# Expert loop of a decoder layer: larger rings for gathered rows and outputs, kept in another buffer, and the last routed groups' sends placed earlier

## Chip, cores and metric

The kernel runs on one core of a Trainium2 chip. The metric is device time in microseconds (us) of one execution; the figure of a kernel is the median of its runs. The engines of the core are named as the profile names them: PE (matmul; PEld its weight loads), DVE (vector), ACT (scalar), POOL (GpSimd) and SP, which here only issues DMAs.

## What is computed

64 sequences of 64 tokens, 128 features each, in float32. Three stages, each added to its input and layer-normed: causal self-attention with 16 query heads and one key/value head, cross-attention on a context of 96 features, and a mixture of experts in which each token goes to two of eight experts. The change is in the third stage. Its reference, shortened:

```python
scores = einsum('bsd,nd->bsn', x, Wr) + br
w = softmax(scores)
_, idx = top_k(scores + biases_N, 2)
val = take_along_axis(w, idx); val = val / sum(val)
h = einsum('md,ndh->nmh', x, Wl1) + bl1          # N=8 experts, D=128, 2H=512
y = einsum('nmh,nhd->nmd', silu(h[..., :256]) * h[..., 256:], Wl2) + bl2
out = einsum('mn,nmd->md', expert weights (val at idx, else 0), y)
x = layernorm(x + out)
```

## The kernel before

The 4096 tokens are T = 32 tiles of 128, kept in `X`. Self-attention and cross-attention go over the tiles in software pipelines; each engine's program is written out by hand in the order in which it runs, and engines wait for each other on semaphores.

**Routing** goes by groups of GT = 4 tiles (G = 8 groups, 0 to 7). When cross-attention has finished the four tiles of a group, PE transposes and scores them, DVE picks the two experts and computes each token's place in the bucket of its expert, and POOL sends the rows: eight indirect DMAs per group (`send(g, n)`, L623), 128 rows of 130 words each, from `xg` to `xbuf` in HBM. One row carries the token's features, the number of its output row and its gate. There is a single `xg`; the routing of a group waits until the group before it has been sent entirely (`route_rows` on ACT, `gate_row` on DVE, `route_ids` on POOL).

**The expert loop** has J = 71 tiles of 128 bucket rows. All engines run `slot_tile(i)` for i from -4 or so to 74. For tile t: SP loads its rows from `xbuf` into a ring `xin` of XB = 12 places (`load_rows`, L443, 65 KB) four slots ahead, and the first-layer weights of its expert into `w_now` (`load_weights`, L448, 256 KB) three slots ahead; both are on SP's one queue, rows(t) ahead of weights(t-1). PE transposes the rows (`x_T_slot`, L1804) in slot t-2, multiplies with `w_now` (`layer1`, L1814, eight records) in slot t, and with the second layer's weights (`layer2`, L1824 and L1826) in slot t+2. ACT copies the transposed rows (`x_copy`, L879), applies SiLU (L887) and, in slot t+3, writes the gated output into a ring `yb` of YB = 8 places (`y_out`, L895). POOL scatters it to `zbuf` in HBM in slot t+3 (`put`, L633, 64 KB, an indirect DMA whose row numbers are read from `xin`).

So a place of `xin` is free when the put of that tile has landed: `load_rows(t)` waits for put t-12, `y_out(t)` for put t-8. Each put counts on one of eight semaphores, `put{t % YB}`. `xin` lies in `KT` and `yb` in `PT`, two buffers of cross-attention.

**Two tables** tell SP which expert and rows each tile has. Table A covers tiles 0 to 39 (J_A = 40) and is computed from groups 0 to 5; the loop may start when these have been sent. SP then waits for `b["s"]` (cross-attention's scores of the tiles up to 30 are done with `KT`; L457). Table B covers tiles 40 to 70: `load_rows(40)` waits (L435) until all groups, 6 and 7 too, have been sent, and for table B. Group 7's routing goes on in the slots of the loop: its places are computed in slots 12 and 13, its gates in slots 14 and 15, its eight sends are in POOL's program in the slots that `LAST_SENDS` gives. Group 6's sends are at the last two steps of cross-attention, `cross(T+1)` and `cross(T+2)`, and, by `LATE_SENDS`, in slots of the loop. `tiles_in_turn` mixes the last steps of cross-attention with the first slots: POOL runs cross(T), slots 0 and 1, cross(T+1), slot 2, cross(T+2), slot 3 and so on.

After the loop SP reads `zbuf` back, PE adds it to `X`, and the last layer norm goes out.

Of the kernel before, what the change touches and what calls it, by code (L numbers as in the profile page):

```python
# [32 lines left out]
D = 128  # L33
# [10 lines left out]
def later(t, n):  # L44

    return t >= n if isinstance(t, int) else True


def decoder(nc, x, ctxT, g1, wqT, wkvT, woutT, g2, xwq, xwk, xwvT, xwo, bo, wrT, br, wl1, bl1, wl2, bl2, bN, out, xbuf, zbuf):
    TOK = x.shape[0]  # L50
    T = TOK // P
# [4 lines left out]
    GT = 4  # L56
    G = T // GT
# [4 lines left out]
    K2 = 2  # L62
    G_A = G - 2
    J_A = (K2 * G_A * GN - NE * (P - 1)) // P
    J = K2 * TOK // P + NE - 1
    JB = 4
    NOWHERE = 1 << 30
    ROW = D + 2
    XB = 12
    EB = 8  # L70
    YB = 8
    NVO = HEADS * D // HW
    HVO = HEADS // NVO

# [1 line left out]
    with ctx:  # L76
# [3 lines left out]
        def sem(name):  # L80
# [20 lines left out]
        arena = sb("arena", [P, 4 * W + DH])  # L101
# [31 lines left out]
        yS = sb("yS", [P, D])  # L133
# [10 lines left out]
        KT = sb("KT", [P, 2, NBLK, P])  # L144
        VBD = sb("VBD", [P, 2, PB, NBLK, P])
        PR = sb("PR", [P, 2, W])
        PT = sb("PT", [P, W])
# [60 lines left out]
        pastB = PR[:, 0, 0:(J - J_A) * (NE - 1)].rearrange("p (j e) -> p j e", j=J - J_A)  # L208
        over = xn[:, :, :].rearrange("p a d -> p (a d)").rearrange("p (e t) -> p e t", e=NE)
        til_to = yS[:, 0:NE * NE].rearrange("p (a e) -> p a e", a=NE)  # L210
        xin = KT[:, :, :, :].rearrange("p a b c -> p (a b c)")[:, 0:XB * ROW]\
            .rearrange("p (b d) -> p b d", b=XB)
        yb = PT[:, :].rearrange("p (b d) -> p b d", b=YB)
        gT = stage[:, :].rearrange("p (b h) -> p b h", b=2)
        VBD_z = VBD[:, :, :, :, :].rearrange("p a b c d -> p (a b c d)")
        z_pair = [v.rearrange("p (t k d) -> p t k d", t=2 * GT, k=K2) for v in (
# [28 lines left out]
        def staging(n):  # L245
# [3 lines left out]
        a = {n: sem("a_" + n) for n in (  # L249
            "stats", "rstd", "xn", "xT_ps", "xT", "xhi", "xlo", "kv", "q", "sq", "vS", "v0", "v1", "ssq", "pow",  # L250
            "cap", "qn", "kn", "knT", "kT", "qT_ps", "qT", "s", "exp", "sum", "norm", "pT_ps", "pT",
            "o", "oT", "y", "yS", "y1", "yrstd", "yn", "yr", "z1", "zrstd", "x1")}

        b = {n: sem("b_" + n) for n in (
            "vo", "vo_hi", "vo_lo", "ctx", "chi", "clo", "xs", "xT_ps", "xhi", "xlo", "q", "qT",
            "k", "kT0", "kT1", "kT2", "kT3", "u", "u0", "u1", "u2", "u3", "s", "max", "sub", "exp", "norm", "sum",
            "pT_ps", "pT", "y", "r", "rb", "z1", "zrstd", "x2")}
# [36 lines left out]
        def place_bank(g):  # L294
            return 1 if g == G - 1 else 4

        LATE_SENDS = {2: 2, 4: 4, 6: 5, 8: 6, 10: 7}
        LAST_SENDS = {16: 0, 19: 1, 22: 2, 24: 3, 27: 4, 30: 5, 32: 6, 34: 7}

        def T_at(g):  # L300
            return GT * g + 6
# [32 lines left out]

        def put_wait(eng, t):

            eng.wait_ge(hs[f"put{t % YB}"], 16 * (t // YB + 1))

        def numbers(eng_type, table, most, t, known):

# [69 lines left out]
        def _(sp):  # L410
# [43 lines left out]

            sent_all(sp, G_A)
            sp.wait_ge(f["tableA"], TABLE_A)
            sp.wait_ge(b["s"], 2 * (T - 1))  # L457
            for i in range(-4, J + 4):
                slot_tile(i, i % JB)

            z_v = zbuf.rearrange("(p t k) d -> p t k d", p=P, k=K2)
            out_v = out.rearrange("(t p) d -> p t d", p=P)
            for t in range(J - YB, J):
                put_wait(sp, t)
            for g in range(G):
                sp.dma_start(z_group[g], z_v[:, g * GT:(g + 1) * GT, :, :]).then_inc(o[f"z{g}"], 16)
# [7 lines left out]
        def _(pool):  # L474
# [103 lines left out]
            def cross(i, p):  # L578
                if p == 0 and has(i + 2):
                    fetch(i + 2, 0)  # L580
                    fetch(i + 3, 1)
                g = (i - GT * 2 - 1) // GT
                sends = {1: (0, 1, 2), 2: (3, 4, 5), 3: (6, 7)}.get(i - GT * 2 - GT * g, ())
                if not 0 <= g < G_A:
                    sends = ()
                if i == T + 1:
                    sends = (0, 1)
                late = p == 1 and has(i)
                if sends:
                    send(g, sends[0])  # L590
                stage_of(b_weights if late else cross_tail, i, p, 1 if late else 3)
                if sends:
                    send(g, sends[1])
                stage_of(cross_tail if late else b_weights, i, p, 3 if late else 1)
                if len(sends) > 2:
                    send(g, sends[2])
                if i == T + 2:
                    send(G - 2, 3)
                if i == 0:
                    body(T + 1, 1)  # L600
                    body(T + 2, 0)
                if i == 1:
                    body(T + 3, 1)
                if (g := due(i, places_at)) is not None:
                    route_ids(g)
# [9 lines left out]
            def send(g, n):  # L615
                if n == 0:
                    pool.wait_ge(f["slot"], g + 1)
                    pool.wait_ge(f["gate"], g + 1)
                    pool.wait_ge(f["xg"], K2 * (g + 1))
                    pool.wait_ge(f["ids"], g + 1)  # L620
                tt, k = n // K2, n % K2
                at = bass.IndirectOffsetOnAxis(ap=slot[:, g % 2, k, tt:tt + 1], axis=0)
                nc.gpsimd.indirect_dma_start(out=xbuf, out_offset=at, in_=xg[:, k, tt, :], in_offset=None)\  # L623
                  .then_inc(f[f"sent{g % 2}"], 16)
# [4 lines left out]

            def put(t, q):  # L630
                pool.wait_ge(hs["yb"], t + 1)
                at = bass.IndirectOffsetOnAxis(ap=xin[:, t % XB, D:D + 1].bitcast(U32), axis=0)
                nc.gpsimd.indirect_dma_start(out=zbuf, out_offset=at, in_=yb[:, t % YB, :], in_offset=None,  # L633
                                             bounds_check=K2 * TOK - 1, oob_is_err=False).then_inc(hs[f"put{t % YB}"], 16)

            def slot_tile(i, q):
                of_tile(put, i, q, 3)
# [1278 lines left out]
```

## Time and profile before

| what | value |
|---|---|
| median of 3 runs | 839.33 us (838.63 to 840.02) |
| the profiled execution | 841.96 us, of which its span is 840.2 us |
| PE busy | 773.7 us, 92% of the span |
| DVE, ACT, POOL busy | 620.4, 596.3, 453.9 us |
| expert loop | about 679 to 809 us of the span |

The span is what the profiler saw from the first to the last instruction; 1.8 us lie around it. An engine's busy share is over three unlike stages, so the rows further down are from single stretches: timelines (one row for each instruction or run of like instructions), the chain of work that ended last, and windows. Brackets in a timeline hold the time that the engine sat idle just ahead and what ended it.

### The profile page before, as it was taken

What the parts mean: (1) busy time and instruction counts of PE and PEld (TensorE: products, weight loads), DVE (VectorE), ACT (ScalarE), POOL (GpSimd) and SP (SyncE); (2) the same over time, 40 slices, a digit from 0 to 9 for tenths busy, and PEclk for the clock granted to TensorE, in tenths of its full rate; (3) what the DMA queues carried; (4) which work ended last, traced back from release to release, by engine and by line L of the source; (5) the groups of instructions that cost most, each with busy time, mean ns of one, the idle gap of its engine ahead of it and who ended that gap; (6) DMA issues with size and microseconds to landing.
All of it is one profiled execution on the core that took longest, in us unless ns stands there. A gap on an engine that the chain in (4) does not pass through costs nothing.

```text
span 840.2 us, 26506 instructions
## 1 busy us (share of the span) xinstructions
PE 773.7 (92%) x9308; PEld 648.0 (77%) x9308; DVE 620.4 (74%) x1834; ACT 596.3 (71%) x1444; POOL 453.9 (54%) x442
## 2 busy tenths in 40 slices
PE   3789999999999998999899999999999888979995
PEld 3578777877877876788888888888888688969962
DVE  4867878778878875789878788888888965634425
ACT  2668888878878865777677777777767567746735
POOL 6466776776776762222253535353544447775643
PEclk9899999999999999999999999999999989998998
DMA  8399999100000000000000000000000057767746
GB/s 271 75 151 159 157 160 156 18 0 0 0 0 0 0 4 1 7 7 7 7 28 11 26 13 22 17 22 16 20 20 19 21 158 221 242 199 227 243 154 225
DMA packets 69392, 64.79 MB, mean 77 GB/s; under 512 B 5702, under 2 KB 54985, under 8 KB 69168
## 3 DMA queue, kind: packets, MB, share of 16 engines
q1 hardware_dynamic: 62592, 51.42, 30.2%
q0 software_dynamic: 4624, 9.61, 3.3%
q10 hardware_dynamic: 2080, 2.49, 0.9%
q8 instruction: 59, 0.97, 0.5%
q14 instruction: 37, 0.30, 0.1%
HBM read 35.37 MB, written 28.58 MB: 76 GB/s over the span
## 4 chain that ended last, share of the span: by engine, by line
PE 40%; issue 22%; POOL 17%; DVE 9%; ACT 6%; DMA 4%; SPq 1%; POOLq 0%; ACTq 0%; DVEq 0%
POOL rq L534 7%; PE bank L1710 6%; PE bank L1814 5%; PE bank L1510 5%; PE bank L1512 4%; PE bank L1511 4%; POOL PR L539 3%; PE bank L1824 2%; PE bank L1698 2%; ACT VBD L393 2%; PE bank L1685 2%; POOL rs L548 2%; POOL rs L544 2%; POOL rs L477 2%; PE bank L1586 1%
## 5 line engine op out<-in xcount | busy, mean ns | idle before, releaser
L393 ACT COPY VBD<-bank 64x512 f32<-64x512 f32 x192 | 111.2, 579 | 28.2 <-PE bank L1512 25.4
L571 POOL TENSOR_TENSOR PR<-PR,rL 128x1024 f32<-128x1024 f32 x32 | 60.9, 1903 | 108.7 <-DVE rL L1120 108.5
L534 POOL TENSOR_TENSOR rq<-ssq,mhalf 128x17 f32<-128x17 f32 x32 | 99.2, 3101 | 16.9 <-DVE ssq L969 16.4
L539 POOL TENSOR_TENSOR PR<-PR,rL 128x1024 f32<-128x1024 f32 x32 | 60.9, 1904 | 82.4 <-DVE rL L1000 82.4
L633 POOL DMA_INDIRECT zbuf<-PT,KT x71 | 69.8, 984 | 36.7 <-issue 20.7
L623 POOL DMA_INDIRECT xbuf<-xg,slot x64 | 64.8, 1012 | 34.0 <-DVE xg L1315 21.4
L1814 PE MATMUL bank<-xT,w_now 128*128 128x128 f32 x568 | 78.1, 282 | 4.1 <-DMA w_now<-in_wl 2.7
L1441 DVE SCALAR_TENSOR_TENSOR stage<-bank,b_now,early 128x128 f32<-128x128 f32 x142 | 43.3, 346 | 46.8 <-ACT early L887 35.3
L1814 PEld LDWEIGHTS bank<-xT,w_now 128*128 128x128 f32 x568 | 71.0, 196 | 6.0 <-ACT xT L879 3.2
L887 ACT ACTIVATE early<-bank,b_now 128x128 f32<-128x128 f32 x142 | 44.5, 365 | 37.9 <-PE bank L1814 37.5
L1710 PE MATMUL bank<-VBD,PT 128*64 128x128 f32 x1024 | 64.5, 280 | 3.2 <-ACT PT L803 3.2
L1710 PEld LDWEIGHTS bank<-VBD,PT 128*64 128x64 f32 x1024 | 56.8, 139 | 11.8 <-ACT PT L803 9.7
L1594 PE MATMUL bank<-arena 128*128 128x128 f32 x512 | 62.8, 275 | 1.2 <-ACT arena L729 0.7
L1586 PE MATMUL bank<-PT,VBD 128*128 128x512 f32 x128 | 63.4, 617 | 0.0
L803 ACT ACTIVATE PT<-bank 128x512 f32<-128x512 f32 x64 | 38.3, 600 | 34.6 <-PE bank L1698 33.9
L1594 PEld LDWEIGHTS bank<-arena 128*128 128x128 f32 x512 | 59.8, 192 | 2.2 <-ACT arena L729 1.6
L576 POOL TENSOR_TENSOR rs<-ve,mhalf 128x1 f32<-128x1 f32 x32 | 18.5, 579 | 71.8 <-DVE ve L1135 71.4
L1510 PE MATMUL bank<-vo_lo,cT_hi 96*128 96x512 f32 x128 | 54.8, 428 | 2.4 <-DVE VBD L393 1.5
L1107 DVE TENSOR_REDUCE mx<-bank 128x8 f32<-128x512 f32 x64 | 43.7, 683 | 17.2 <-PE bank L1685 17.0
L713 ACT ACTIVATE PR<-bank 128x512 f32<-128x512 f32 x64 | 34.7, 594 | 29.2 <-PE bank L1564 29.2
L969 DVE TENSOR_REDUCE ssq<-arena 128x17 f32<-128x1088 f32 x32 | 41.2, 1288 | 12.9 <-ACT arena L677 5.2
L1512 PE MATMUL bank<-vo_hi,cT_hi 96*128 96x512 f32 x128 | 50.4, 394 | 0.0
(253 smaller groups left out, 2316.1 us busy)
## 6 DMA issues: line engine op xcount, KB each, us to landing
w_now<-in_wl SPq DMA_DIRECT2D x71, 256.0 KB
xbuf<-blank SPq DMA_DIRECT2D x1, 17160.0 KB, 121.6
KT<-xbuf SPq DMA_DIRECT2D x71, 65.0 KB
VBD<-zbuf SPq DMA_DIRECT2D x4, 512.0 KB, 5.1
out<-X SPq DMA_DIRECT2D x8, 256.0 KB, 2.3
cT<-in_ctxT ACTq DMA_DIRECT2D x16, 96.0 KB, 2.0
zbuf<-PT,KT POOLq DMA_INDIRECT x71, 3.2
wl_sb<-in_wl POOLq DMA_DIRECT2D x1, 1024.0 KB, 9.0
```

The costliest lines, as they stand in the source:

```text
L393: u = copy(VBD[h * SEQ:(h + 1) * SEQ, p, s, lo:lo + blocks, :], bank[CHUNK_BANK[c]][s * SEQ:(s + 1) * SEQ, :].rearrange("k (a d) -> k a d" ...
L534: nc.gpsimd.tensor_tensor(rq[:, :], ssq[:, :], mhalf[:, 0:HEADS + 1], ALU.pow).then_inc(a["pow"], 1)
L539: nc.gpsimd.tensor_tensor(v, v, rL[:, p, :].unsqueeze(2).broadcast_to([P, HEADS, SEQ]), ALU.mult)\
L571: nc.gpsimd.tensor_tensor(v, v, rL[:, p, :].unsqueeze(2).broadcast_to([P, HEADS, SEQ]), ALU.mult)\
L623: nc.gpsimd.indirect_dma_start(out=xbuf, out_offset=at, in_=xg[:, k, tt, :], in_offset=None)\
L633: nc.gpsimd.indirect_dma_start(out=zbuf, out_offset=at, in_=yb[:, t % YB, :], in_offset=None, bounds_check=K2 * TOK - 1, oob_is_err=False) ...
L1510: M(out_, l_hi, r_lo, start=True, stop=False)
L1512: return M(out_, l_hi, r_hi, start=False, stop=True)
L1586: M(bank[4 + s][:, :], VBD[:, p, s, 0, :], PT[:, s * HW:(s + 1) * HW], start=True, stop=True)\
L1594: m = M(bank[0][:, 0:D], OT[:, k, :], wout_sb[:, k, :], start=(k == 0), stop=(k == NBLK - 1))
L1710: m = M(bank[bk][s * SEQ:(s + 1) * SEQ, 0:D], PT[:, k * P + s * SEQ:k * P + (s + 1) * SEQ], VBD[:, p, s, k, :], start=(k == 0), stop=(k == ...
L1814: m = M(bank[2 + q % 2][:, c * P:(c + 1) * P], w_now[:, q, c * P:(c + 1) * P], xT[:, q % 2, :], start=True, stop=True)
```

## The change

The ring `xin` grows from 12 to 16 places and `yb` from 8 to 12; both lie in `arena`, which holds self-attention's output weights and work space. SP's wait for `b["s"]` becomes one for `a["yS"]` (self-attention's last output has left the banks). The number of put semaphores stays eight and is now NPUT, apart from YB; so that two puts never count on one semaphore at a time, POOL waits for put t-8 to have landed ahead of put t. The sends of groups 5, 6 and 7 are placed earlier in POOL's program.

```diff
-    XB = 12
+    XB = 16
     EB = 8
-    YB = 8
+    YB = 12
+    NPUT = 8
...
-        xin = KT[:, :, :, :].rearrange("p a b c -> p (a b c)")[:, 0:XB * ROW]\
-            .rearrange("p (b d) -> p b d", b=XB)
-        yb = PT[:, :].rearrange("p (b d) -> p b d", b=YB)
+        xin = arena[:, 0:XB * ROW].rearrange("p (b d) -> p b d", b=XB)
+        yb = arena[:, XB * ROW:XB * ROW + YB * D].rearrange("p (b d) -> p b d", b=YB)
...
-        LATE_SENDS = {2: 2, 4: 4, 6: 5, 8: 6, 10: 7}
-        LAST_SENDS = {16: 0, 19: 1, 22: 2, 24: 3, 27: 4, 30: 5, 32: 6, 34: 7}
+        LATE_SENDS = {3: 7}
+        LAST_SENDS = {16: 0, 18: 1, 20: 2, 22: 3, 24: 4, 26: 5, 28: 6, 30: 7}
...
-            eng.wait_ge(hs[f"put{t % YB}"], 16 * (t // YB + 1))
+            eng.wait_ge(hs[f"put{t % NPUT}"], 16 * (t // NPUT + 1))
...
-            sp.wait_ge(b["s"], 2 * (T - 1))
+            sp.wait_ge(a["yS"], T)
...
                 sends = {1: (0, 1, 2), 2: (3, 4, 5), 3: (6, 7)}.get(i - GT * 2 - GT * g, ())
                 if not 0 <= g < G_A:
                     sends = ()
+                if g == G_A - 1:
+                    sends = {1: (0, 1, 2, 3), 2: (4, 5, 6, 7)}.get(i - GT * 2 - GT * g, ())
                 if i == T + 1:
-                    sends = (0, 1)
+                    sends = (0, 1, 2, 3)
...
-                if len(sends) > 2:
-                    send(g, sends[2])
+                for n in sends[2:]:
+                    send(g, n)
                 if i == T + 2:
-                    send(G - 2, 3)
+                    for n in (4, 5, 6):
+                        send(G - 2, n)
...
             def put(t, q):
                 pool.wait_ge(hs["yb"], t + 1)
+                if later(t, NPUT):
+                    put_wait(pool, t - NPUT)
```

What this does to POOL's program shows at three places. The first is the end of cross-attention, at group 5's last sends (`xbuf<-xg,slot` is a send, `PR<-PR,rL` the scaling of a tile's attention weights, `rs<-ve,mhalf` a layer norm's power). Before:

```order
L576 TENSOR_TENSOR rs<-ve,mhalf 128x1 [waits b_z1]
L623 DMA xbuf<-xg,slot 33792x130
L571 TENSOR_TENSOR PR<-PR,rL 128x1024 [waits b_sum]
L623 DMA xbuf<-xg,slot 33792x130 x2
L571 TENSOR_TENSOR PR<-PR,rL 128x1024 [waits b_sum]
L623 DMA xbuf<-xg,slot 33792x130
L576 TENSOR_TENSOR rs<-ve,mhalf 128x1 [waits b_z1] x2
```

and with the change:

```order
L576 TENSOR_TENSOR rs<-ve,mhalf 128x1 [waits b_z1]
L626 DMA xbuf<-xg,slot 33792x130
L571 TENSOR_TENSOR PR<-PR,rL 128x1024 [waits b_sum]
L626 DMA xbuf<-xg,slot 33792x130 x2
L571 TENSOR_TENSOR PR<-PR,rL 128x1024 [waits b_sum]
L576 TENSOR_TENSOR rs<-ve,mhalf 128x1 [waits b_z1] x2
```

The last send of group 5 stood behind the scaling of tile 30; now both sends that end the group stand ahead of it. The number of sends ahead of it in these rows is the same since send 4 has moved up by one power, out of them.

The second place is where the loop begins on POOL, from the first send of group 6 on (`zbuf<-PT,KT` and `zbuf<-arena` are puts). Before:

```order
L623 DMA xbuf<-xg,slot 33792x130 [waits f_xg,f_ids,f_gate,f_slot]
L576 TENSOR_TENSOR rs<-ve,mhalf 128x1 [waits b_z1]
L623 DMA xbuf<-xg,slot 33792x130 x2
L576 TENSOR_TENSOR rs<-ve,mhalf 128x1 [waits b_z1]
L623 DMA xbuf<-xg,slot 33792x130
L633 DMA zbuf<-PT,KT 8192x128 [waits h_yb] x2
L623 DMA xbuf<-xg,slot 33792x130
L633 DMA zbuf<-PT,KT 8192x128 [waits h_yb] x2
L623 DMA xbuf<-xg,slot 33792x130
```

and with the change:

```order
L626 DMA xbuf<-xg,slot 33792x130 [waits f_xg,f_ids,f_gate,f_slot]
L576 TENSOR_TENSOR rs<-ve,mhalf 128x1 [waits b_z1]
L626 DMA xbuf<-xg,slot 33792x130 x3
L576 TENSOR_TENSOR rs<-ve,mhalf 128x1 [waits b_z1]
L626 DMA xbuf<-xg,slot 33792x130 x3
L638 DMA zbuf<-arena 8192x128 [waits h_yb]
L626 DMA xbuf<-xg,slot 33792x130
L638 DMA zbuf<-arena 8192x128 [waits h_yb] x7
L638 DMA zbuf<-arena 8192x128 [waits h_put0,h_yb]
```

Four of group 6's sends (4 to 7) stood between pairs of puts; three now stand ahead of the first put and one behind it, and from put 8 on each put has a second wait.

The third place is the end of group 7's sends on POOL. Before, its last five:

```order
L623 DMA xbuf<-xg,slot 33792x130
L633 DMA zbuf<-PT,KT 8192x128 [waits h_yb] x3
L623 DMA xbuf<-xg,slot 33792x130
L633 DMA zbuf<-PT,KT 8192x128 [waits h_yb] x3
L623 DMA xbuf<-xg,slot 33792x130
L633 DMA zbuf<-PT,KT 8192x128 [waits h_yb] x2
L623 DMA xbuf<-xg,slot 33792x130
L633 DMA zbuf<-PT,KT 8192x128 [waits h_yb] x2
L623 DMA xbuf<-xg,slot 33792x130
L633 DMA zbuf<-PT,KT 8192x128 [waits h_yb] x39
```

and with the change its last two:

```order
L626 DMA xbuf<-xg,slot 33792x130
L638 DMA zbuf<-arena 8192x128 [waits h_put0,h_yb]
L638 DMA zbuf<-arena 8192x128 [waits h_put1,h_yb]
L626 DMA xbuf<-xg,slot 33792x130
L638 DMA zbuf<-arena 8192x128 [waits h_put2,h_yb]
L638 DMA zbuf<-arena 8192x128 [waits h_put3,h_yb]
```

Between two sends there are always two puts now. The last send stood behind put 31 and stands behind put 27. The programs of PE, ACT, DVE and SP have the same instructions in the same order as before.

## Rows read from the trace of the kernel before

**Rows 1.** Windows of 20 us: busy us by engine, clock share, DMA share, GB/s.
```profile
660.00:680.00 20.00, 15.86 (x183) 13.13 (x182) 15.77 (x53) 13.43 (x25) 6.04 (x6) 0.83 0.27 78
...
740.00:760.00 20.00, 14.63 (x105) 13.78 (x105) 5.78 (x22) 8.47 (x30) 12.10 (x13) 0.84 0.62 187
```

**Rows 2.** Chain that ended last: start us, us, what.
```profile
747.28 2.31 DMA xbuf<-xg,slot
749.66 0.52 SPq L342
...
751.50 3.03 DMA w_now<-in_wl
```

**Rows 3.** Timeline of PE: start us, us, line, operation, count, [idle].
```profile
684.87 1.16 PE L1814 MATMUL bank<-xT,w_now 128*128 128x128 f32 x8
...
749.76 0.22 PE L1826 MATMUL bank<-b_part,ones_b 128*128 x1
752.84 0.33 PE L1804 MATMUL bank<-ident,KT 128*128 128x128 f32 x1 [2.86 <-DMA KT<-xbuf]
754.67 2.04 PE L1814 MATMUL bank<-xT,w_now 128*128 128x128 f32 x8 [1.50 <-DMA w_now<-in_wl]
...
760.51 1.06 PE L1814 MATMUL bank<-xT,w_now 128*128 128x128 f32 x8
...
762.02 1.06 PE L1814 MATMUL bank<-xT,w_now 128*128 128x128 f32 x8
```

**Rows 4.** Timeline of POOL in the expert loop.
```profile
690.84 1.00 POOL L633 DMA_INDIRECT zbuf<-PT,KT  x1 [0.30 <-issue]
692.14 0.99 POOL L633 DMA_INDIRECT zbuf<-PT,KT  x1 [0.30 <-issue]
...
704.99 0.96 POOL L623 DMA_INDIRECT xbuf<-xg,slot  x1 [0.30 <-issue]
706.26 0.99 POOL L633 DMA_INDIRECT zbuf<-PT,KT  x1 [0.31 <-ACT PT L895]
...
711.09 1.00 POOL L633 DMA_INDIRECT zbuf<-PT,KT  x1 [1.07 <-ACT PT L895]
...
747.28 0.97 POOL L623 DMA_INDIRECT xbuf<-xg,slot  x1 [0.30 <-issue]
```

**Rows 5.** Timeline of PE where cross-attention ends and the loop begins.
```profile
672.25 0.45 PE L1804 MATMUL bank<-ident,KT 128*128 128x128 f32 x1 [2.64 <-DMA KT<-xbuf]
...
673.46 1.06 PE L1698 MATMUL bank<-ident,PR 128*128 128x128 f32 x4
675.26 3.54 PE L1710 MATMUL bank<-VBD,PT 128*64 128x128 f32 x32 [0.75 <-ACT PT L803]
...
682.98 1.97 PE L1710 MATMUL bank<-VBD,PT 128*64 128x128 f32 x32 [0.80 <-ACT PT L803]
```

**Rows 6.** Timeline of POOL there: the last sends of group 5, the first of group 6.
```profile
655.40 1.01 POOL L623 DMA_INDIRECT xbuf<-xg,slot  x1 [0.17 <-issue]
656.72 0.96 POOL L623 DMA_INDIRECT xbuf<-xg,slot  x1 [0.31 <-issue]
...
666.23 1.01 POOL L623 DMA_INDIRECT xbuf<-xg,slot  x1 [0.16 <-issue]
...
681.52 1.06 POOL L623 DMA_INDIRECT xbuf<-xg,slot  x1 [2.16 <-DVE xg L1315]
...
688.68 0.57 POOL L576 TENSOR_TENSOR rs<-ve,mhalf 128x1 f32<-128x1 f32 x1 [1.88 <-DVE ve L1135]
```

**Rows 7.** Timeline of DVE there: table A's last step, tile 31's subtraction.
```profile
658.18 0.18 DVE L1362 CAST row_tab<-row_f 128x40 int32<-128x40 f32 x1
...
671.73 0.69 DVE L1111 TENSOR_TENSOR PR<-bank,mx 128x512 f32<-128x512 f32 x1
```

**Rows 8.** Timeline of ACT there, just ahead of the first slot's copy.
```profile
670.66 0.23 ACT L867 ACTIVATE ex<-sh 128x32 f32<-128x32 f32 x1
```

**Rows 9.** Puts (line L633) from 690 us on: time from issue to landing.
```profile
DMA to landing us min/median/max: 2.2/3.2/4.4
```

More of the change, by code:

```diff
@@ L462, in _ @@
             out_v = out.rearrange("(t p) d -> p t d", p=P)
-            for t in range(J - YB, J):
+            for t in range(J - NPUT, J):
                 put_wait(sp, t)
@@ L631, in put @@
                 pool.wait_ge(hs["yb"], t + 1)
+                if later(t, NPUT):
+                    put_wait(pool, t - NPUT)
                 at = bass.IndirectOffsetOnAxis(ap=xin[:, t % XB, D:D + 1].bitcast(U32), axis=0)
                 nc.gpsimd.indirect_dma_start(out=zbuf, out_offset=at, in_=yb[:, t % YB, :], in_offset=None,
-                                             bounds_check=K2 * TOK - 1, oob_is_err=False).then_inc(hs[f"put{t % YB}"], 16)
+                                             bounds_check=K2 * TOK - 1, oob_is_err=False).then_inc(hs[f"put{t % NPUT}"], 16)
             def slot_tile(i, q):
```

## Prediction

> **What bounds the kernel now.** I first read the windows of 20 us. Through cross-attention and the loop PE is busy nearly all the time; it loses time in two windows, 660 to 680 (15.9 of 20 us busy) and 740 to 760 (14.6), and in both the granted clock of TensorE averages 0.83 and 0.84, so a part of them ran at its lower level [rows 1]. What holds PE there is in the timeline of PE and the chain of waits.
>
> The second hole is the larger. PE has ended slot 38's work at 749.98, waits 2.86 us for the rows of tile 40, then 1.50 us for the weights of tile 39, and starts that tile at 754.67. Two tiles later it is 760.51: 5.84 us for two tiles at the lower level, where a tile takes 1.51 us at the full one (760.51 to 762.02) [rows 3]. The chain leads from there back through SP to group 7's last send, issued at 747.28 and landed 2.31 us later; then come two table reads, the row load, and the weight load, issued at 751.50 [rows 2]. That send was late because POOL had a queue: from put 0 at 690.84 to it POOL issues one indirect DMA after another, nearly all with 0.30 us between them and no other releaser [rows 4]. So from put 0 to slot 39 the time is POOL's, not PE's: 32 puts and twelve sends. PE's holes ahead of 750 cost nothing, since PE arrives there early anyway.
>
> The first hole is where the loop begins. PE stands 2.64 us at the first tile's transpose, until 672.25, for rows from `xbuf` [rows 5]. SP could not load them before group 5's last send, issued at 666.23 [rows 6]. PE then runs at the lower level: the 32 matmuls of L1710 take 3.54 us where the same take 1.97 a little later [rows 5].
>
> **Part 1, group 5's sends.** In POOL's program send 6 and 7 move ahead of tile 30's scaling. Before, sends 5 and 6 start back to back, at 655.40 and 656.72, and send 7 sits behind a scaling that waits for DVE, at 666.23 [rows 6]. Now send 4 goes into a gap further up, and sends 5, 6 and 7 take the places of 4, 5 and 6, so the last one is at 656.72. With 2.3 us to land [rows 2] that is 659.0. Table A is ready at 658.36 [rows 7]. From the landing, near 668.5, to PE's transpose at 672.25 it took 3.7 us before, so the rows are there at about 663, while PE wants them at 669.6 (672.25 less 2.64). SP's other wait, for cross-attention's scores or now for self-attention's output, is over long before, in both kernels; it costs nothing. So this wait goes entirely.
>
> What is late next? ACT has the copy of the transposed rows in its queue and is free for it at 670.89 [rows 8]; the second transpose follows at about 671.4. PE's next four matmuls wait for DVE's first subtraction of tile 31, ready at 672.42 [rows 7]. So they start at 672.5 and not at 673.46, last 0.6 and not 1.06, and after ACT's copy (0.75) L1710 starts at about 673.8 and not at 675.26: 1.45 us. If the clock stays full, for the idle time is in three short pieces now, L1710 ends 1.57 us sooner on top. The step from there to tile 31's L1710, before at 682.98, is carried by PE: I take 3.0 us for the shift of everything at the start of the loop, with 1.45 as the low end (clock falls all the same) and 3.6 as the high one (with 0.6 us of the waits gone at the second L1710, 0.80 before [rows 5]).
>
> **Part 2, group 6's sends.** The first, before at 681.52, waits for DVE's gate [rows 6] and comes 3.0 us sooner, at 678.5. Sends 1 to 3 fit ahead of the next power (L576), which waits for tile 31 and moves from 688.68 [rows 6] to 685.7. Behind it stand now three sends, put 0 and send 7, at POOL's pitch of 1.29 us (690.84 to 692.14; a send and a put 704.99 to 706.26, 1.27) [rows 4]. The power takes 0.57 and a gap of 0.2, then come sends 4, 5, 6 at 686.45, 687.75, 689.05, put 0 at 690.35, send 7 at 691.65, put 1 at 692.95. Before, put 1 was at 692.14 [rows 4]: POOL is 0.8 us behind the old time there, with four sends less to go.
>
> **Part 3, group 7's sends.** From put 1 to the last send POOL has had 30 puts, four sends of group 6 and eight of group 7, 42 intervals in 55.14 us (692.14 to 747.28), of them 1.07 us of idle ahead of put 13 [rows 4], at the point where ACT stood for group 6's last send. The rest is 54.07 / 42 = 1.287 us each. Now there are 26 puts and eight sends: 34 x 1.287 = 43.8 us, and 0.3 for the step at put 13, whose cause is gone, for group 6 is out by 694. That holds only while POOL has a queue: outputs come at PE's 1.51 us a tile, behind a loop that starts 3.0 us sooner, and put 13 would be ready near 706 against 709 in POOL's queue, put 27 near 727 against 736. It holds.
>
> **Part 4, the wait of each put for put t-8.** Eight puts lie at least 8 x 1.29 = 10.3 us apart, and a put lands within 4.4 us [rows 9], so no put waits. The price is that of a second semaphore on an instruction. The nearest rows: a put, with one wait, takes 1.29 us and a send, with none, 1.27 [rows 4], so 0.02 each; 20 puts (8 to 27) make 0.4 us. Ends: nothing, and 2 us. The Trainium skill gives, in Advanced Engine Details and Errata, Network/Comms, 50 to 100 ns for a sequencer's reading of a semaphore; by that the 20 waits would be 1 to 2 us, and the result 0.6 to 1.6 us later. No row here shows it.
>
> **Part 5, the rings.** Seen alone they remove SP's waits for put t-12 and ACT's for put t-8. With POOL up to 9 us behind (put 27), the old rings would bind now: `load_rows(39)` would wait for put 27, the new one waits for put 23, at 728.4, landed by 733; PE wants these rows at 738. So the rings earn nothing by themselves and keep part 3 from being lost. That the data lie in `arena` costs nothing.
>
> **Sum.** Last send: 692.95 + 43.8 + 0.3 + 0.4 = 737.45, against 747.28: 9.8 us. From there on the chain is as before: 2.3 us to land, table reads, rows, weights, 7.4 us from send to tile 39 [rows 2, 3], at 744.85. Would PE be there? Tile 2 starts at 684.87 [rows 3] less 3.0, and slot 38's end is 37 tiles of 1.51 us later, 737.8; the 18 matmul records of group 7's routing, at 14 records a tile an estimate of 1.9 us, make it 739.7. The rows of tile 40 come at 743.0. So PE still waits, 3.3 us and 1.5 us, and the clock falls as before. POOL stays what decides, and up to 3.3 us of small stalls of PE ahead of it cost nothing. Behind tile 39 the same 32 tiles and the same end follow. The profiled execution would be 841.96 - 9.8 = 832.2 us; the median of before lies 2.6 us under its profile, and the same difference gives 839.33 - 9.8 = **829.5 us**.
>
> **Rivals.**
> - *The clock falls at the loop's start all the same.* Then the shift is 1.45 and not 3.0: 831.0. For it: PE still idles 3 of the 4.2 us from 669.6 on, in pieces. Against: the level fell with a hole of 2.64 us in one piece [rows 5], and the pieces now are under 1.5. Chance 0.2, own range 830.3 to 832.
> - *POOL is dearer:* the second wait costs up to 0.1 us or the chain of group 6 slips; the last send comes 2 to 4 us later than summed: 831.5 to 833.5. Chance 0.12.
> - *More is won:* PE's wait is shorter and the clock doesn't fall behind tile 39. That would give back 5.84 - 3.02 = 2.8 us: 826.7. The wait of rows and weights is, by the sum, no shorter than before, which speaks against. Chance 0.1.
> - *The sends move, but nothing comes of it:* SP's load of tile 40 is really held by table B. DVE computes it in slots 17 to 23, far ahead of slot 36; the chain shows the send as the last releaser [rows 2]. Same time, 838.5 to 840. Chance 0.02.
> - *Slower.* The wait for put t-8 blocks POOL. SP, freed from its short ring, loads further ahead, the DMA queues fill, and puts land long after the 4.4 us of now. From put 0 to put 27 there are 36 intervals of 1.29 us, so eight puts and the sends among them are 36 / 27 x 8 x 1.29 = 13.7 us on average, and the wait comes round 27 / 8 = 3.4 times: each microsecond of landing above 13.7 costs 3.4. It decides from landings of 13.7 + 9.8 / 3.4 = 16.6 us; at 18 us the last send is 14.6 us late and the kernel at 844. The Trainium skill's page DMA: Bandwidth & Descriptors (Anatomy of one DMA) says that completion into HBM "can cause a surprisingly long delay". Against: 4.4 us is the longest of 71 puts with the DMA engines at 0.62 in the busier window [rows 1, 9], and SP still runs only four slots ahead. Chance 0.04.
>
> **How the numbers follow.** Forecast 0.52, own range 828.3 to 830.3 (shift 2.2 to 3.6, second waits 0 to 0.8 us, part 3's idle 0.2 to 1). The range that leaves out no more than 2 in 10 takes in the first rival, most of the second and most of the third: 826.7 to 832.8. Differences under 0.2% (1.7 us) can't be told from no change here. Faster 0.94, same 0.02, slower 0.04.
>
> **What would show it.** In the changed profile: group 5's last send near 656.7 and no wait of PE for rows near 670; a clock of 1.00 there; put 1 near 693; POOL without idle time from put 0 to the last send, near 737.5, 1.29 us apiece; a hole of PE of about 5 us that ends near 745, with the lower clock behind it. I would be wrong if puts are more than 1.35 us apart, if POOL idles between 693 and 737, if PE itself is late at tile 40, or if SP's load of tile 40 follows something other than that send.

## The result, and the profile after

The changed kernel takes **833.19 us** (median of 6 runs, 829.74 to 834.02), beside 839.67 us for the kernel before in the same set: ratio 0.9906, 95% interval 0.9887 to 0.9925, 6.3 to 9.5 us gained. That ratio is not the quotient of the two medians, which is 0.9923, or 6.5 us; the interval holds both. A second set gave 832.98 beside 840.92, ratio 0.9910 (0.9886 to 0.9934). The forecast was 829.5 from a gain of 9.8 us; the gain is 7.6 to 7.9 by the ratios, 6.5 and 7.9 by the medians. Reckoned from the median of before that the forecast started from, the ratio gives 839.33 x 0.9906 = 831.4 us, inside its range of 826.7 to 832.8; with 6.5 us it is 832.9, at the range's upper end, and the two medians themselves (832.98 and 833.19) lie 0.2 and 0.4 above it. All of them lie outside the narrower range of 828.3 to 830.3.

The profiled execution took 833.86 us, its span 832.1. Of the 8.1 us that it lies under the span of before, not all is the change's. The work is alike up to POOL's scaling of tile 29, and that scaling already starts 1.86 us sooner:

```profile
640.59 1.90 POOL L571 TENSOR_TENSOR PR<-PR,rL 128x1024 f32<-128x1024 f32 x1 [4.19 <-DVE rL L1125]
```

Before, it started at 642.45. Over the thirteen profiles of this study it starts between 638.8 and 643.0, the two ends in kernels that have all code up to there in common. In this pair the difference arises in the first 60 us (windows 20 to 30: clock 0.67 before and 0.83 after; 50 to 60: PE busy 7.40 and 9.23). So I take **the start of that scaling as an anchor**: every place below is given as the time since it. To the end of the span it was 197.75 us before, 191.51 after (6.2 less), and 190.36 in the second profile of the changed kernel (7.4 less).

**The start of the loop.** Timeline of PE, after (start us, us, line, operation, count, [idle before <- what ended it]); it answers to [rows 5]:

```profile
668.86 0.33 PE L1809 MATMUL bank<-ident,arena 128*128 128x128 f32 x1 [1.08 <-ACT VBD L393]
669.84 0.38 PE L1809 MATMUL bank<-ident,arena 128*128 128x128 f32 x1 [0.65 <-ACT xT L884]
670.71 1.09 PE L1703 MATMUL bank<-ident,PR 128*128 128x128 f32 x4 [0.49 <-DVE PR L1116]
672.55 3.68 PE L1715 MATMUL bank<-VBD,PT 128*64 128x128 f32 x32 [0.75 <-ACT PT L808]
...
680.62 1.97 PE L1715 MATMUL bank<-VBD,PT 128*64 128x128 f32 x32 [0.80 <-ACT PT L808]
```

The wait for rows is gone: what ends PE's idle time at the first transpose is ACT now, not a DMA. But the four matmuls of L1703 take 1.09 us and the 32 of L1715 3.68, the durations at the lower level. Windows, after (busy us by engine, then clock share, DMA share, GB/s); the forecast had put 1.00 there:

```profile
669.00:672.00 3.00, 1.66 (x6) 0.85 (x5) 2.93 (x6) 1.57 (x5) 0.00 (x0) 0.66 0.37 104
672.00:675.00 3.00, 2.45 (x24) 2.46 (x26) 2.56 (x8) 2.98 (x6) 0.91 (x2) 0.50 0.12 36
```

The second L1715 starts 140.03 us after the anchor; before it was 140.53 [rows 5, and 642.45]. The loop starts 0.5 us sooner, not 3.0. One pair can't give the 0.5 exactly. In the four profiles with group 5's sends where they were this matmul comes at 139.87 to 140.84 after the anchor, and in the seven with them moved and no extra matmuls on PE at 139.32 to 140.30, on average 0.7 us sooner.

**POOL.** Timeline after, answering to [rows 4] and [rows 6]: last send of group 5, put 0, put 1, put 13, last send of group 7.

```profile
654.88 0.96 POOL L626 DMA_INDIRECT xbuf<-xg,slot  x1 [0.30 <-issue]
...
691.02 1.00 POOL L638 DMA_INDIRECT zbuf<-arena  x1 [0.30 <-issue]
692.33 0.97 POOL L626 DMA_INDIRECT xbuf<-xg,slot  x1 [0.30 <-issue]
693.60 0.99 POOL L638 DMA_INDIRECT zbuf<-arena  x1 [0.30 <-issue]
...
707.14 1.00 POOL L638 DMA_INDIRECT zbuf<-arena  x1 [0.75 <-ACT arena L900]
...
738.21 0.97 POOL L626 DMA_INDIRECT xbuf<-xg,slot  x1 [0.30 <-issue]
```

From put 1 to the last send it takes 44.61 us; before 55.14. The last send comes 97.62 us after the anchor and not 104.83: 7.2 us gained there.

**The hole at tile 39.** The chain that ended last (start us, us, what), answering to [rows 2], and PE's timeline, answering to [rows 3]:

```profile
738.21 3.67 DMA xbuf<-xg,slot
...
741.94 0.67 SPq L342
...
743.92 3.27 DMA w_now<-in_wl
```

```profile
745.14 0.33 PE L1809 MATMUL bank<-ident,arena 128*128 128x128 f32 x1 [0.80 <-DMA arena<-xbuf]
747.32 1.13 PE L1819 MATMUL bank<-xT,w_now 128*128 128x128 f32 x8 [1.85 <-DMA w_now<-in_wl]
...
749.62 1.91 PE L1819 MATMUL bank<-xT,w_now 128*128 128x128 f32 x8
...
752.20 1.06 PE L1819 MATMUL bank<-xT,w_now 128*128 128x128 f32 x8
```

PE now waits 0.80 + 1.85 = 2.65 us, where it was 2.86 + 1.50 = 4.36. The lower level comes later and for less long: two tiles take 4.88 us (747.32 to 752.20), not 5.84. But the last send takes 3.67 us to land, not 2.31.

### The profile page after: what moved, and what is told of

Same layout as the page of the kernel before. It is cut to its first block, busy times and chain, and to the rows that moved or that the text cites. A ratio compares the mean times of both kernels' runs of the same rounds, so it can differ in the third digit from the quotient of the medians.

```text
span 832.1 us, 26529 instructions
## 1 busy us (share of the span) xinstructions
PE 770.5 (93%) x9276; PEld 646.4 (78%) x9308; DVE 620.7 (75%) x1834; ACT 596.5 (72%) x1444; POOL 454.3 (55%) x442
## 4 chain that ended last, share of the span: by engine, by line
PE 47%; issue 19%; POOL 13%; DVE 9%; ACT 6%; DMA 3%; SPq 1%; POOLq 0%; DVEq 0%; ACTq 0%
PE bank L1715 7%; PE bank L1819 6%; PE bank L1515 5%; POOL rq L534 5%; PE bank L1517 5%; PE bank L1516 5%; POOL PR L539 3%; PE bank L1829 3%; PE bank L1703 3%; PE bank L1591 2%; PE bank L1599 2%; PE bank L1690 2%; ACT VBD L393 2%; DMA w_now<-in_wl 2%; POOL rs L548 1%
## 5 line engine op out<-in xcount | busy, mean ns | idle before, releaser
L638 POOL DMA_INDIRECT zbuf<-arena x71 | 69.8, 983 | 31.6 <-issue 21.2
L1715 PE MATMUL bank<-VBD,PT 128*64 128x128 f32 x1024 | 64.7, 280 | 3.2 <-ACT PT L808 3.2
L1715 PEld LDWEIGHTS bank<-VBD,PT 128*64 128x64 f32 x1024 | 56.8, 139 | 11.8 <-ACT PT L808 9.8
L1112 DVE TENSOR_REDUCE mx<-bank 128x8 f32<-128x512 f32 x64 | 43.8, 684 | 17.3 <-PE bank L1690 17.0
L1516 PE MATMUL bank<-vo_hi,cT_lo 96*128 96x512 f32 x128 | 50.4, 394 | 0.0
```

The costliest lines, as they stand in the source:

```text
L1516: M(out_, l_lo, r_hi, start=False, stop=False)
L1715: m = M(bank[bk][s * SEQ:(s + 1) * SEQ, 0:D], PT[:, k * P + s * SEQ:k * P + (s + 1) * SEQ], VBD[:, p, s, k, :], start=(k == 0), stop=(k == ...
```

## Experiments

The times since the anchor, all from profiles; the ratio, with its interval, is to the kernel before in the same set, from several executions of each. The quotients of the plain medians differ from it by up to 0.002 (the change 0.9923, group 5 0.9993, group 7 0.9936, one send a slot 0.9866), each inside its interval.

| kernel | last send | end of span | ratio (95%) |
|---|---|---|---|
| before | 104.83 | 197.75 | 1 |
| the change | 97.62 | 191.51 | 0.9906 (0.9887 to 0.9925) |
| the change, again | 97.51 | 190.36 | 0.9910 (0.9886 to 0.9934) |
| rings only | 105.48 | 197.99 | 0.9988 (0.9969 to 1.0007) |
| sends only | 98.00 | 192.46 | 0.9937 (0.9916 to 0.9958) |
| group 5's sends only | 102.97 | 195.49 | 0.9984 (0.9965 to 1.0003) |
| group 6's sends only | 103.32 | 195.63 | 0.9976 (0.9960 to 0.9993) |
| group 7's sends only | 99.45 | 192.78 | 0.9946 (0.9926 to 0.9966) |
| change, PE kept busy | 96.48 | 188.93 | 0.9905 (0.9874 to 0.9936) |
| change, one send a slot | 88.81 | 186.58 | 0.9880 (0.9850 to 0.9909) |
| the same, again | 87.99 | 187.01 | 0.9863 (0.9839 to 0.9887) |
| one send a slot, PE kept busy | 87.37 | 185.23 | 0.9891 (0.9865 to 0.9918) |
| one send a slot, old rings | 87.70 | 192.51 | 0.9946 (0.9925 to 0.9967) |

Two profiles of one kernel differ by 0.1 to 0.8 us at the send and 0.4 to 1.2 at the end, so a difference of about 1 us at the end settles nothing by itself.

### Rings alone, sends alone

My theory was that the rings earn nothing alone and only keep what the sends win. The rival was that the rings carry a part of it.

```diff
# rings only, against before: rings, place, waits of the change; sends as before
+    XB = 16
+    YB = 12
+    NPUT = 8
+        xin = arena[:, 0:XB * ROW].rearrange("p (b d) -> p b d", b=XB)
# sends only, against before: all sends of the change; rings as before
+        LATE_SENDS = {3: 7}
+        LAST_SENDS = {16: 0, 18: 1, 20: 2, 22: 3, 24: 4, 26: 5, 28: 6, 30: 7}
```

> The larger rings in arena, the second wait of each put and SP's other wait as in the change, all sends where they were before. Theory (POOL's queue of puts and sends, ended by group 7's last send, is what the stretch up to tile 39 waits for; the rings earn nothing alone): same as before within 1 us, last send of group 7 near its old place, 56 us behind put 0. Rival (the rings free SP's loads and so feed PE sooner): 3 to 8 us faster than before.

> All sends as in the change, but the rings as before (12 and 8 places, in KT and PT, no second wait on puts). Theory: POOL has a queue all the same; row loads follow puts, PE is slowed to POOL's pace near slot 38, but tile 39 starts when the last send has landed, so the gain is that of the change, 6 to 8 us, or at most 1.5 us less. Rival (the prediction's part 5: the old rings bind and part 3 is lost): 2 to 4 us less gained than by the change, with SP waiting for puts over 10 us in the loop's first part.

Rings alone: last send 105.48, end 197.99, within a profile's spread of before, and a ratio that can't be told from 1. Sends alone: end 192.46, 5.3 us under before, 1 to 2 above the change; by the ratios (0.9937 and 0.9906 to 0.9910) 2.3 to 2.6. So the rings are worth 1 to 2.6 us, and only beside the sends. By the ratios that is more than the 1.5 us of my theory, and nearer to the rival. How they are worth it shows in what SP waits for between 690 and 760 us (what, us in total, times, longest). Sends only, and then the change:

```profile
SPq L338 <- DMA zbuf<-PT,KT: 15.4, 14, 3.1
```

```profile
SPq L448 <- PE bank L1819: 13.4, 27, 1.2
SPq L435 <- DMA xbuf<-xg,slot: 3.6, 1, 3.6
```

With the old rings SP waits for puts fourteen times and comes so late to tile 40 that it no longer waits for the last send at all. PE then has small waits spread over the loop in place of one hole.

### The three groups of sends, each alone

```diff
# group 7 only, against before
-        LAST_SENDS = {16: 0, 19: 1, 22: 2, 24: 3, 27: 4, 30: 5, 32: 6, 34: 7}
+        LAST_SENDS = {16: 0, 18: 1, 20: 2, 22: 3, 24: 4, 26: 5, 28: 6, 30: 7}
# group 6 only, against before
-        LATE_SENDS = {2: 2, 4: 4, 6: 5, 8: 6, 10: 7}
+        LATE_SENDS = {3: 7}
-                    sends = (0, 1)
+                    sends = (0, 1, 2, 3)
-                    send(G - 2, 3)
+                    for n in (4, 5, 6):
+                        send(G - 2, n)
# group 5 only, against before
+                if g == G_A - 1:
+                    sends = {1: (0, 1, 2, 3), 2: (4, 5, 6, 7)}.get(i - GT * 2 - GT * g, ())
```

> The kernel before with group 7's sends alone moved, as in the change. Theory: the last send has four puts less ahead of it, 4 x 1.29 = 5.2 us; it comes about 100 us behind the scaling of tile 29 (104.8 before, 97.6 in the changed kernel), and the end 4 to 5.5 us sooner than before. Rival (the moves of groups 5 and 6 carry the gain): under 2 us.

> The kernel before with group 6's sends alone moved, as in the change. Theory: the number of sends and puts ahead of group 7's last one stays but for one send that goes into an idle gap (1.3 us), and ACT's stand for group 6's last send in slot 13 (1.5 us) goes: the last send and the end come 1 to 2 us sooner than before, the whole time the same within its interval. Rival (four sends between the first puts hold back the loop): over 3 us sooner.

> The kernel before with group 5's sends alone moved (send 4 into an earlier gap, sends 5 to 7 ahead of tile 30's scaling, slots' code behind them as before). Theory, after the other runs: the last send of group 5 comes some 9.6 us sooner against the start of that scaling, PE's wait of 2.64 us for rows goes, but the granted clock falls at the first slots all the same, so tile 31's 32 matmuls (L1710 of before) move by only 0.5 us, the last send of group 7 by 0 to 0.6 us, and the end likewise, a ratio of 0.9995 to 1.0. With the other parts alone (group 7's sends 5.0, group 6's 2.1, rings none, all against that anchor) this closes the sum of 6.2 for the whole change to within the half microsecond that two profiles of one kernel differ by. Rival, my step on record: 3.0 us of shift, of which the queue of POOL passes on what it does not lose; then the last send comes 2 to 3 us sooner, a ratio of 0.997. Rival two: group 5 alone makes it slower, because POOL's four sends ahead of the scaling of tile 30 delay the first slots' rows: then the last send comes later, a ratio over 1.001.

Group 7 alone brings the last send 5.4 us forward and the end 5.0. Four puts fewer ahead of the send at 1.29 us make 5.2. From put 1 to the send it is 4.7 us less (50.41 against 55.14), since POOL stood 0.4 us longer ahead of put 13 (1.47 against 1.07); the other 0.65 us are an earlier put 1. The 5.0 at the end is not that send passed on, though. With the old rings SP stood for puts and came to tile 40 only 3.3 us behind the send, which then took some 5.5 us to land. Group 7 only, what SP waited for at tile 40, and PE's timeline (tiles 36, 39 and 41):

```profile
SPq L435 <- DMA xbuf<-xg,slot: 2.2, 1, 2.2
```

```profile
744.30 1.13 PE L1814 MATMUL bank<-xT,w_now 128*128 128x128 f32 x8 [2.29 <-DMA w_now<-in_wl]
...
749.07 1.13 PE L1814 MATMUL bank<-xT,w_now 128*128 128x128 f32 x8
...
752.18 1.06 PE L1814 MATMUL bank<-xT,w_now 128*128 128x128 f32 x8
```

Tile 39 starts 110.25 us after the anchor, 2.0 sooner than before (112.22). The rest is the clock: it stayed at 1.00 from 744 to 753, and the two tiles from 749.07 take 3.11 us, not 5.84. PE's hole is now at tile 36, whose rows had waited for put 24 and whose weights took 6.05 us to land.

Group 6 alone brings 1.5 at the send and 2.1 at the end. Group 5 alone brings 1.9 at the send and 2.3 at the end, between my two expectations (0 to 0.6, and 2 to 3). Its start of the loop shows why it is more than the change's own 0.5. Timeline of PE, group 5 only:

```profile
672.72 0.63 PE L1700 MATMUL bank<-ident,PR 128*128 128x128 f32 x4 [0.62 <-DVE PR L1113]
674.24 3.00 PE L1712 MATMUL bank<-VBD,PT 128*64 128x128 f32 x32 [0.89 <-DVE r L1126]
...
681.93 1.97 PE L1712 MATMUL bank<-VBD,PT 128*64 128x128 f32 x32 [0.80 <-ACT PT L805]
```

The same idle pieces, but the level falls some 1.5 us later: the four transposes still take 0.63 us, the 32 matmuls 3.00, and tile 31's come 139.32 us after the anchor, 1.2 sooner than before. The second profile of one send a slot is such a case too (0.63, 3.33, 139.41); both of the change are not (1.09, 3.68, 140.03 and 139.95). By the ratios the parts come to 1.3 + 2.0 + 4.5 us, and 1.0 for the rings: 8.8, where the whole is 7.6 to 7.9, a difference inside the intervals. By the anchor they come to 9.2 (2.3 + 2.1 + 5.0 - 0.2), where the whole is 6.2 to 7.4. The last send's landing is a part of it that differs from kernel to kernel: 2.3 us with group 5 or 6 alone, some 5.5 with group 7 alone, 3.7 with all of them. The rest stays open.

### Does the clock at the loop's start decide?

PE gets filler matmuls in its idle pieces around the first slots, which write a bank that nobody reads; they are not part of the computation.

```diff
# change, PE kept busy, against the change
+            def filler(n):
+                pe.wait_ge(b["u0"], T)
+                for _ in range(n):
+                    M(bank[7][:, :], ident_b[:, :], causal[:, :, :].rearrange("q h k -> q (h k)"), start=True, stop=True)
                 if i == T:
+                    filler(4)
                     slot_tile(-2, -2 % JB)
+                    filler(2)
                     slot_tile(-1, -1 % JB)
+                    filler(3)
...
+                if i == T:
+                    filler(3)
                 stage_of(b_y, i, p, 2)
```

> The changed kernel with twelve extra matmuls (128x512, bf16, into a bank that nobody reads then) in PE's idle pieces where cross-attention ends. They are filling and not part of the result. Theory (the shift at the loop's start came out at 0.5 us and not 3.0 because TensorE went to its lower level in spite of the shorter pieces of idle time): granted clock 1.00 throughout 667 to 677, tile 31's L1715 about 2.0 to 2.5 us sooner against the scaling of tile 29 than in the changed kernel, last send as much sooner, 2 to 2.5 us faster than the changed kernel, 9.5 to 10.5 us faster than before. Rival (what follows waits for DVE and ACT anyway): clock kept, but under 0.7 us gained on the changed kernel.

Timeline of PE, change with PE kept busy:

```profile
669.59 0.63 PE L1703 MATMUL bank<-ident,PR 128*128 128x128 f32 x4
670.05 0.81 PE L1753 MATMUL bank<-causal,ident_b 128*128 128x512 bf16 x3
671.11 1.97 PE L1715 MATMUL bank<-VBD,PT 128*64 128x128 f32 x32 [0.24 <-DVE r L1129]
...
678.38 1.97 PE L1715 MATMUL bank<-VBD,PT 128*64 128x128 f32 x32 [1.80 <-ACT PT L808]
```

The clock stays at 1.00 in all windows from 669 to 681, and the first L1715 takes 1.97. So the fall was brought on by the idle pieces, which the extra matmuls filled. But tile 31's comes only 1.1 us sooner than in the change (138.91 against 140.03), not 2 to 2.5: PE, faster now, waits 1.80 us there. The wait is ACT's queue. Timelines of DVE and of ACT, same kernel:

```profile
674.02 1.42 DVE L1302 CAST slot<-slot_f 128x8 uint32<-128x8 f32 x1
```

```profile
676.64 0.62 ACT L892 ACTIVATE early<-bank,b_now 128x128 f32<-128x128 f32 x2 [1.53 <-DVE b_now L1437]
677.16 1.08 ACT L808 ACTIVATE PT<-bank 128x512 f32<-128x512 f32 x2
```

ACT has SiLU of tile 1 ahead of the copy of `PT`, and SiLU waits for the bias that DVE writes behind group 6's places; one cast of DVE among them takes 1.42 us here, 0.17 in the change. At full clock DVE and ACT are next in line. At the last send 1.0 to 1.1 us remain, at the end 1.4 to 2.6; the ratio, 0.9905, can't be told from the change's. So the theory's 2 to 2.5 us did not come, and the rival's reason (DVE and ACT) did.

### What if POOL's queue were out of the way?

```diff
# change, one send a slot, against the change
-        LAST_SENDS = {16: 0, 18: 1, 20: 2, 22: 3, 24: 4, 26: 5, 28: 6, 30: 7}
+        LAST_SENDS = {16: 0, 17: 1, 18: 2, 19: 3, 20: 4, 21: 5, 22: 6, 23: 7}
# the same with old rings: XB = 12 in KT, YB = 8 in PT, no second wait of the puts
# the same with PE kept busy: the fillers above as well
```

> The changed kernel with group 7's sends in slots 16 to 23, one each, so that the last one stands behind put 20 and not put 27. Theory: last send seven places of 1.29 us sooner, 9 us, landed near slot 33, before SP comes to tile 40; PE has no hole at tile 39 and no low clock behind it; then POOL's own queue of 71 puts and 9 sends is the bound, about 80 x 1.29 us from put 0 to the last put: 6 to 9 us faster than the changed kernel, 14 to 17 us faster than before. Rival (PE or the row loads behind late puts bound it then): a new hole of PE near slot 30 and under 4 us gained on the changed kernel.

> One send per slot in 16 to 23, with the rings of before (12 and 8 places, in KT and PT, no second wait). Theory: with POOL up to 11 us behind, the rows of tile 34 wait for put 22, which lands near 736 where PE wants them near 731: PE loses 4 to 6 us in slots 26 to 36, so this is 3 to 5 us slower than the same with the large rings. Rival (the rings earn nothing here either): within 1 us of it.

> Group 7's sends in slots 16 to 23, one each, and the twelve filling matmuls at the end of cross-attention, together. Theory: the two gains add, since PE and not POOL's queue is the bound now and the loop starts 2.5 us sooner: counted from the scaling of tile 29 the end comes 7 to 8 us sooner than in the changed kernel (4.9 and 2.6), 14 us sooner than before; whole time 0.982 to 0.985 of before. Rival (POOL's queue of 71 puts and 9 sends, 80 x 1.29 us behind put 0, takes over as the bound): the gain stops at 5 to 6 us on the changed kernel.

With one send in each slot the last one is issued 8.8 us sooner than in the change, and from 720 to 752 us PE has this one wait left:

```profile
728.91 1.13 PE L1819 MATMUL bank<-xT,w_now 128*128 128x128 f32 x8 [0.49 <-DMA w_now<-in_wl]
```

The hole at tile 39 and the lower clock behind it are gone; SP's wait at L435 too. The end comes 4.9 us sooner than in the change, not 8.8 (3.4 when the second profiles of both are compared): the rest is PE's own work. I had expected 6 to 9 us in the whole time; the ratios of this set say 2.2, the comparison further down 3.6. It was PE that bound it, not POOL's queue, and of the rival's new hole near slot 30 only that one wait of 0.49 us showed. Here the rings do matter. With the old ones the last send is as early (87.70), but the end is 5.9 us later (5.5 against the second profile; I had expected 3 to 5), and PE waits 4.9 us in this stretch in eight pieces. PE, one send a slot with the old rings, three of eight waits from 720 to 752:

```profile
730.47 1.13 PE L1818 MATMUL bank<-xT,w_now 128*128 128x128 f32 x8 [1.44 <-DMA w_now<-in_wl]
...
734.48 1.13 PE L1818 MATMUL bank<-xT,w_now 128*128 128x128 f32 x8 [0.75 <-DVE stage L1445]
...
746.33 1.13 PE L1818 MATMUL bank<-xT,w_now 128*128 128x128 f32 x8 [0.96 <-DMA w_now<-in_wl]
```

The fillers on top bring the end to 185.23, 1.4 us less in the profile (6.3 under the change, where I had expected more) and nothing in the ratio.

### The change and one send a slot, side by side

> The change itself once more, on one chip with the kernel before and with the version of one send per slot. Expected: ratio to the kernel before 0.990 to 0.993 (its first interval was 0.9887 to 0.9925, and its parts measured alone give less than their sum). In the profile, against the start of POOL's scaling of tile 29: last send of group 7 at 97.6 and end of span at 191.5, each within 0.7. Rival: the first profile was an unlucky one, with one landing of 3.67 us for the last send, where the kernel before has 2.31; then this profile lands it in 2.3 us and ends 1.4 us sooner, at 190.1, and PE's idle time ahead of tile 39 is 1.3 us and not 2.65.

> The change with group 7's sends in slots 16 to 23, one in each slot, once more beside the change on one chip, since the two were so far compared only by way of the kernel before (0.9880 and 0.9906, with intervals that overlap). By the two profiles it ends 4.9 us sooner than the change when both are measured from POOL's scaling of tile 29: so a median 3 to 5 us under the change's, a ratio to the kernel before lower by 0.004 to 0.006, an end at 186.6 after that scaling. Rival: PE's and POOL's paths are both near their limits here, and what the hole at tile 39 gives back is lost in small waits in most executions; then the medians are within 1.7 us.

Medians 832.98 and 829.43: **one send a slot is 3.6 us faster than the change** and 11.5 faster than before (ratio 0.9863). My rival for the landing fell: the last send took 3.75 us in the second profile as well. The end came at 190.36 all the same, 1.1 us sooner than expected and outside the 0.7 that I had allowed, with PE idle for 2.06 us ahead of tile 39. The windows over these landings show what differs. The first is of before, the second of the change, the third of the change again:

```profile
747.30:749.60 2.30, 2.30 (x23) 2.29 (x23) 0.74 (x4) 1.24 (x5) 1.94 (x2) 1.00 0.19 59
```

```profile
738.20:741.90 3.70, 3.70 (x37) 3.68 (x36) 1.94 (x8) 2.99 (x11) 2.93 (x3) 1.00 0.64 209
```

```profile
737.20:740.90 3.70, 3.70 (x37) 3.67 (x37) 1.71 (x8) 2.98 (x11) 2.88 (x3) 1.00 0.67 201
```

Before, SP had issued its last load 4.2 us ahead of the send and stood waiting, so the DMA engines were nearly idle (0.19). Now SP arrives there at the same moment as POOL: its load of tile 38's weights, 256 KB, goes out 0.25 us ahead of the send in the first profile and 0.19 behind it in the second. Timeline of SP, after:

```profile
737.96 0.33 SPq L448 DMA_DIRECT2D w_now<-in_wl  x1
743.40 0.33 SPq L443 DMA_DIRECT2D arena<-xbuf  x1
```

It is the same over all profiles. Eight have sends on their chains: seven sends with the DMA share at 0.09 to 0.18 landed in 2.31 to 2.35 us, seven at 0.58 to 0.80 in 3.01 to 4.08, and group 7's last send alone, at 0.84, took some 5.5. One of the slow ones is group 6's last send in the kernel before (share 0.78), so the forecast could have read it there. Chain, before:

```profile
704.99 3.67 DMA xbuf<-xg,slot
```

I did not try to hold the weight load back, so that it makes the difference is read from the shares, not shown by an experiment.

## Why the forecast was right, and where its sizes were off

- **What bounds it.** Right: POOL's queue up to the last send, then the chain to tile 39. Group 7's sends alone give at the send, within 0.4 us, what the count of puts says. The figure came into the range with some luck. The 831.4 us are close to the first rival's 831.0, but by other sums: its shift was to cost 1.55 us and cost 2.5, the chain lost 1.7 more, and 0.7 to 1.6 us came back behind tile 39.
- **Part 1: the step that failed.** "If the clock stays full, for the idle time is in three short pieces now": the pieces came as forecast (1.08, 0.65, 0.49 and 0.75 us, all under 1.5) and the clock fell all the same. The term was 3.0 us and measured 0.5 to 0.6 in the two profiles of the change. Even my low end of 1.45 was too high: it had the four matmuls of L1703 at the full level, 0.6 us, and they took 1.09. So the first L1715 starts 0.85 sooner (131.96 after the anchor against 132.81), runs 0.14 longer (3.68 and 3.54), and the way from its end to tile 31's takes 0.21 longer: 0.50. The first rival had the mechanism. Had the clock stayed, it would have been about 1.6 (PE kept busy: 138.91 against 140.53), since ACT and DVE are next. "What is late next?" was answered for the first L1715 and not for tile 31's.
- **Part 2.** Put 1 was to come 0.8 us later than before. It comes 3.3 later (153.01 against 149.69 after the anchor), all of the 2.5 from part 1's shift.
- **Part 3.** Right: 44.61 us from put 1 to the last send, against 43.8 + 0.3 + 0.4 = 44.5. Two of these terms were off and cancel: the 0.4 for second waits is not there, and POOL stood 0.75 us ahead of put 13, where I had 0.3. ACT's wait for group 6's last send (1.50 us before) is gone as forecast, but its copy of group 7's rows, 1.15 us, still stands ahead of put 13's output.
- **Part 4.** The second wait costs nothing that can be measured: the mean from one put to the next, leaving out put 13 and one step of 1.49 us, is 1.29 us before (19 steps) and 1.29 after (17). Three puts in a row on POOL's timeline of after, each with two waits, are 1.28 and 1.29 us apart, as puts with one wait were [rows 4]; and no put waited for put t-8. The longest landing is not the 4.4 us that I took, since the chain of before has a put with 5.13 us from the start of its issue (at 726.71); that is still about half of 10.3. By the Trainium skill's 50 to 100 ns for a semaphore's reading (Advanced Engine Details and Errata, Network/Comms) the 20 waits would have been an estimated 1 to 2 us; the trace doesn't agree.
- **Part 5.** Half right. Nothing alone; but with the old rings the sends don't lose what they win, they lose 1 to 2.6 us of it. With one send a slot, where POOL is out of the way, it is 5.5 to 5.9.
- **The chain behind the last send.** It was held at 7.4 us and takes 9.1 (738.21 to 747.32), and 9.0 in the second profile: 1.4 of it the landing, taken from a send with the DMA engines nearly idle. PE was to be ready at 739.7; with small waits of its own on the way it is ready near 744, which cost nothing, as the forecast said of up to 3.3 us, but for making the hole shorter.
- **Sum.** 9.8 us at the send, less 2.5 (part 1), less 0.1, is the 7.2 measured; less 1.7 (chain) is 5.5 at tile 39 (5.8 in the second profile); plus 0.7 to 1.6 behind it, 6.2 to 7.4 at the end. The shorter stretch at the lower level gives 1.0 there (4.88 against 5.84); what makes the difference to 0.7 and to 1.6 is open. The runs say 6.5 to 7.9.

The slower rival (a put blocked by put t-8) did not show. The rows for part 4:

```profile
702.64 0.98 POOL L638 DMA_INDIRECT zbuf<-arena  x1 [0.30 <-issue]
703.92 0.98 POOL L638 DMA_INDIRECT zbuf<-arena  x1 [0.30 <-ACT arena L900]
705.21 0.98 POOL L638 DMA_INDIRECT zbuf<-arena  x1 [0.30 <-issue]
```

## What to carry over

Where one engine's queue of equal steps sets the time, count the steps ahead of the last one that somebody waits for; that count times the pitch was right to 0.1 to 0.4 us, and the order in the queue was worth more than the depth of the rings. Don't take the rest of the chain as fixed when its start moves: what had been issued long before may now be issued beside it, here a weight load beside the last send. A landing time read from a row holds for the DMA load of that row. And a hole cut into short pieces has not saved the clock; what is late next has to be followed up to the place where the shift is claimed.

## What was not expected of the hardware

- The granted clock fell from 2.4 to 1.2 GHz with idle pieces of PE of 1.08, 0.65, 0.49 and 0.75 us between groups of one to four matmuls, as it had with 2.64 us in one piece. From run to run it falls some 1.5 us sooner or later at the same place, which moves tile 31 by 0.7 us, as much as group 5's sends won there.
- A send (an indirect DMA of 128 rows of 520 bytes) lands in 2.3 us with the DMA engines at 0.09 to 0.19, and in 3.0 to 4.1 with them at 0.58 to 0.80 (fourteen sends), once in some 5.5 at 0.84.
- A second semaphore wait on POOL's indirect DMA adds nothing to its pitch of 1.29 us.
- DVE's cast of 128x8 took 1.42 us, not 0.17, where it stood beside a scaling of POOL (673.51 to 675.41) and ended with it. The Trainium skill, SBUF — State Buffer (Who interferes with whom), says that DVE in a two-port mode and POOL hold a shared pair of ports in turn, each for a whole instruction; the trace agrees with that. Five traces have it: in four more the cast starts 0.51 us (one), 1.38, 1.47 and 1.72 us into that scaling of 1.90 us, takes 1.42, 0.54, 0.46 and 0.21 us, and ends with it. In the other eight it starts behind the scaling and takes 0.17. No run was made to test it.
- The start of one program differs by up to 4.2 us within its first 640 us, in kernels with the same code there; two profiles are best compared from a common point just ahead of the change.
